# One core, four layers: paired maximum units on two row halves, earlier key and value projections, an earlier first expert

## The reference

```python
x = x + tanh(g_xattn[0]) * L0_xattn(layernorm(x), ctx)   # 16 heads of 16, causal: first 100 context rows
x = x + tanh(g_ffn[0])   * L0_ffn(layernorm(x))          # 8 experts, best one, and a shared one
x = x + tanh(g_xattn[1]) * L1_xattn(layernorm(x), ctx)   # latent attention, below
x = x + tanh(g_ffn[1])   * L1_ffn(layernorm(x))          # self attention, then 32 experts, best 8, and a shared one

def L1_xattn(hidden_q, kv_c):
    q_hk  = (hidden_q @ Wq.T).reshape(B, S, 16, 128)
    q_big = rope(einsum('bshk,hkq->bshq', q_hk, w_kc_q))
    kv_r  = rope(kv_c)                                   # 8 x 1444 x 64
    scores = einsum('bhsr,bhlr->bhsl', einsum('bshq,hqr->bhsr', q_big, W_qr),
                                       einsum('bld,hdr->bhlr', kv_r, W_kr))
    attn  = softmax(scores)                              # 16 heads x 100 queries over 1444 keys
    ctx_c = einsum('bhsl,bld->bhsd', attn, kv_r)
    return (ctx_lat(ctx_c, w_kc_kv)) @ Wo.T
```

## Time and profile before

| what | value |
|---|---|
| median of 3 runs | 1599.77 us (1599.54 to 1603.27) |
| profiled execution | 1590.53 us |
| its span, first to last instruction | 1588.8 us |
| mean granted TensorE clock | 0.944 of full speed |
| PE busy | 1470.2 us (93%), 7316 products |
| PEld busy | 1102.4 us (69%) |
| DVE busy | 899.7 us (57%) |
| ACT busy | 620.0 us (39%) |
| POOL busy | 781.4 us (49%) |
| DMA | 88.61 MB, mean 56 GB/s |

### The profile page before, as it was taken

How to read it: one execution, slowest core, us unless ns; L and a number is a source line. 1 busy time by engine, 2 the same in 40 slices (tenths; PEclk the granted TensorE clock), 3 DMA queues, 4 the chain that set the end, 5 groups by cost and what they waited for, 6 DMA issues and landing times. The chain is left out here.

```text
span 1588.8 us, 20773 instructions
## 1 busy us (share of the span) xinstructions
PE 1470.2 (93%) x7316; PEld 1102.4 (69%) x7316; DVE 899.7 (57%) x1581; ACT 620.0 (39%) x1117; POOL 781.4 (49%) x605
## 2 busy tenths in 40 slices
PE   7898999899978999999999998978999998799998
PEld 4586565544445766766766665567988877799998
DVE  1573111255556676786776763567878774444444
ACT  2243121133341344344343342356666653333333
POOL 0760102135544897797797764057465541233332
PEclk7798999699997999999999999789999998899999
DMA  8004111611001010110110000200110001343441
GB/s 301 1 1 146 51 47 38 212 48 49 1 11 55 29 57 4 54 57 1 57 57 1 19 1 2 81 27 10 46 54 2 27 1 41 105 122 121 121 121 51
DMA packets 60317, 88.61 MB, mean 56 GB/s; under 512 B 7556, under 2 KB 44612, under 8 KB 60230
## 3 DMA queue, kind: packets, MB, share of 16 engines
q1 hardware_dynamic: 59206, 85.82, 16.9%
q0 software_dynamic: 1024, 1.64, 0.4%
HBM read 81.92 MB, written 5.41 MB: 55 GB/s over the span
## 5 line engine op out<-in xcount | busy, mean ns | idle before, releaser
L965 ACT ACTIVATE prob<-PS 121x800 f32<-121x800 f32 x192 | 158.3, 838 | 248.8 <-PE PS L1937 246.0
L1344 DVE TENSOR_REDUCE mx<-PS 128x1 f32<-128x482 f32 (+1 forms) x312 | 185.6, 649 | 44.7 <-PE PS L1917 43.5
L618 POOL TENSOR_TENSOR e_wl<-e_wf,e_wh 128x768 fp32r<-128x768 f32 x33 | 70.8, 2144 | 181.0 <-ACT e_wh L883 159.1
L695 POOL TENSOR_TENSOR hT<-hT,prob 121x800 f32<-121x800 f32 x56 | 109.3, 1951 | 66.4 <-ACT prob L965 64.3
L1916 PE MATMUL PS<-kth,qs 128*128 128x482 f32 (+1 forms) x312 | 128.6, 412 | 13.4 <-DVE kl L1337 5.8
L1952 PE MATMUL PS<-prob,kvn 121*64 121x400 f32 (+1 forms) x768 | 136.1, 503 | 0.9 <-ACT prob L965 0.9
L695 POOL TENSOR_TENSOR xc<-xc,prob 121x800 f32<-121x800 f32 x56 | 117.7, 2101 | 13.6 <-ACT prob L965 8.3
L1917 PE MATMUL PS<-kl,qm 66*128 66x482 f32 (+1 forms) x312 | 122.5, 393 | 0.0
L1934 PE MATMUL PS<-qs,kth 128*121 128x400 f32 (+1 forms) x384 | 111.6, 373 | 7.8 <-DMA qm<-nml 4.8
L1937 PE MATMUL PS<-qm,kl 66*121 66x400 f32 (+1 forms) x384 | 103.8, 352 | 0.0
L1952 PEld LDWEIGHTS PS<-prob,kvn 121*64 121x64 f32 (+1 forms) x768 | 52.3, 137 | 71.2 <-issue 68.6
(11 more groups left out here) (278 smaller groups left out, 3565.9 us busy)
## 6 DMA issues: line engine op xcount, KB each, us to landing
e_wb<-routing SPq DMA_DIRECT2D x32, 400.0 KB, 3.9
wgu<-in_L_ffn_gate_up_proj SPq DMA_DIRECT2D x8, 1024.0 KB, 14.0
krt<-in_ctx_T SPq DMA_DIRECT2D x8, 722.0 KB, 4.1
ksw<-in_ctx_Tswap SPq DMA_DIRECT2D x8, 722.0 KB, 5.7
wdn<-in_L_ffn_down_proj SPq DMA_DIRECT2D x8, 512.0 KB, 7.9
wq<-in_L_ffn_Wq SPq DMA_DIRECT2D x4, 1024.0 KB, 5.1
wo<-in_L_ffn_Wo SPq DMA_DIRECT2D x4, 1024.0 KB, 5.5
e_wf<-in_L_ffn_Wg SPq DMA_DIRECT2D x32, 128.0 KB, 2.2
```

The source lines that it names most:

```text
L618: pool.tensor_tensor(m["wl"][:, slot], m["wf"][:, slot], m["wh"][:, slot].bitcast(fp32), ALU.subtract).then_inc(ms["wlo"], 1)
L695: pool.tensor_tensor(acc, acc, prob[:, n % RING], ALU.add).then_inc(xb["ap"], 1)
L965: act.activation(prob[0:k, n % RING], PS[0:k, 2 * (n % 2):2 * (n % 2) + 2, 0:GC], ACT.Exp).then_inc(xb["ex"], 1)
L1344: dve.tensor_reduce(mx3[:, m, g:g + 1], PS[:, 4 + k % 3, 0:SEG[g][1]], AX.X, ALU.max).then_inc(xb["free"], 1)
```

## The change

1. Units go in pairs. `queries_keys` takes one or two units: first their high products, then their low ones. `qm2` and `kl2` now have 128 rows, the same content in rows 0 to 63 and 64 to 127, and the second unit's low product reads rows 64 to 127. The low products of units have 64 rows in place of 66. So that the two score rows still exist, DVE sets rows 64 and 65 of `kl2` to one after each batch's maxima (before: once), ACT copies the queries twice (before: once), and `keep` falls away.
2. `UNITS` has more even steps, and in steps 8 and 14 a pair stands behind `values`.
3. The key and value projections move into the first norm, where PE, ACT and DVE have them between the norm's own steps; the context and its weights are loaded ahead of x. POOL expands the first three units of keys and one of values before the attention's stage, and clears `vx` there. The tanh of the gates moves from ACT's first place to behind the query copies.
4. The stage `ST_RT1` is gone. PE goes from the logits straight into the first expert's two `hidden`, turns the routing and opens the sums behind them; ACT keeps the routing between the first expert's gates; DVE waits for the spread routing at the first product that needs it. Logits and turned routing use banks 6, 4 and 5.

```diff
-        kl2 = sb("kl2", [DC + 2, 2, SK], fp32r, stack=st3)
-        qm2 = sb("qm2", [DC + 2, 2, HQ], fp32r, stack=st3)
+        kl2 = sb("kl2", [P, 2, SK], fp32r, stack=st3)
+        qm2 = sb("qm2", [P, 2, HQ], fp32r, stack=st3)
-        UNITS = (0, 0, 0, 0, 2, 4, 6, 8, 11, 14, 16, 18, 21, 24, 27, 30, 31, 33, 36, 39, 39, 39, 39, 39, 39)
+        UNITS = (0, 0, 0, 0, 2, 4, 6, 8, 10, 14, 16, 18, 20, 23, 25, 29, 31, 33, 36, 39, 39, 39, 39, 39, 39)
...
 # SP
+            sp.dma_start(c0T[:], a["ctx0T"]).then_inc(ld_x, 16)
+            sp.dma_start(wkv0T[:], a["L0_xattn_WkvT"]).then_inc(ld_x, 16)
             for c in range(NC):
                 sp.dma_start(xT[:, c, :], ...).then_inc(ld_x, 16)
...
 # ACT
-                act.activation(qm2[:, b % 2], qs[0:DC + 2, b].rearrange("p h s -> p (h s)"), ACT.Copy,
-                               scale=keep[:, 0:1]).then_inc(xb["q2"], 1)
+                src = qs[0:DC, b].rearrange("p h s -> p (h s)")
+                act.activation(qm2[0:DC, b % 2], src, ACT.Copy).then_inc(xb["q2"], 1)
+                act.activation(qm2[DC:P, b % 2], src, ACT.Copy).then_inc(xb["q2"], 1)
...
 # DVE
-                dve.tensor_tensor(kl2[0:DC, b % 2, cols], krt[0:DC, cols], kth[0:DC, b % 2, cols].bitcast(fp32),
+                dve.tensor_tensor(kl2[:, b % 2, cols], krt[:, cols], kth[:, b % 2, cols].bitcast(fp32),
                                   ALU.subtract).then_inc(xb["kl"], 1)
...
                 dve.tensor_tensor(nml[:], PS[0:MT, 4 + k % 3, 0:P], nmh[:].bitcast(fp32), ALU.subtract).then_inc(xb["free"], 1)
+                dve.memset(kl2[DC:DC + 2, b % 2].bitcast(fp32), 1.0).then_inc(xb["one"], 1)
...
 # PE
-                bank = PS[:, next_slot((xb["free"], next(freed))), 0:SEG[g][1]]
-                mm(bank, qs[...][:, cols], kth[:, b % 2, keys], start=True, stop=False)
-                mm(bank, qm2[:, b % 2, cols], kl2[:, b % 2, keys], start=False, stop=True).then_inc(xb["fill"], 1)
+                for u in units:
+                    ...
+                    banks.append(PS[:, next_slot((xb["free"], next(freed))), 0:SEG[g][1]])
+                    mm(banks[-1], qs[...][:, cols], kth[:, b % 2, keys], start=True, stop=False)
+                for i, u in enumerate(units):
+                    ...
+                    rows = slice(DC * i, DC * i + DC)
+                    mm(banks[i], qm2[rows, b % 2, cols], kl2[rows, b % 2, keys], start=False, stop=True).then_inc(xb["fill"], 1)
+
+            def unit_pairs(b, first, end):
+                for u in range(first, end, 2):
+                    queries_keys(b, range(u, min(u + 2, end)))
...
+            means(xT)
+            (4 key products)
+            variances("n0")
+            pe.wait_ge(ns["xc"], 2)
+            values_in(0, 0)
+            values_in(1, 1)
+            pe.wait_ge(p0["ke"], 2 * NC)
+            spread("n0")
+            values_in(2, 6)
+            values_in(3, 7)
...
                         hidden(m, ms, n, k, j, va + j, q, first and k < 2)
+                        if first and k == 1:
+                            routing_turned()
+                            open_sums()
```

175 lines of the change are left out of this document (87 added, 88 removed).

## The result

The changed kernel takes 1736.13 us (median, 1733.84 to 1738.68) where the kernel before, on the same chip, takes 1600.74 (1599.54 to 1603.27): 1.0837 of its time, 95% interval 1.0808 to 1.0866. Slower was forecast, by 25 us; it is 135 us, far outside the range (1592 to 1646). Ratios here compare executions in the same state, which leaves out two far ones, 2403.87 us in `xb_front` (granted clock 0.551) and 3629.33 us in `wait_long`.

What follows compares the result with a forecast made beforehand. PE was taken to bound the latent attention from batch 1 on. Latent attention +37, first stages -6 and first expert -6 gave +25 on 1590.5, 1615.5; with 9.3 carried over, 1625 us, range 1608 to 1642 (8 in 10: 1592 to 1646).

Steps and rivals of the forecast that it cites:

- From batch 1 on PE sets the pace: Latent attention: PE is busy 59.50 of 62 us, so a unit's cost on PE is its cost to the kernel.
- The price of a pair: Latent attention: a pair takes 1.07 us in place of 0.88, low products side by side, 0.20 us per change of form.
- form free: Rival: changes of the array's form cost nothing here, so pairs save time; 1571 us, chance 0.13.
- not side by side: Rival: the low products on row halves don't overlap, 0.21 us more a pair; 1652 us, chance 0.09.
- +27: Latent attention: pairs and single units cost +24 and +8 us, less 5 where column halves already paid a change.
- PE's waits for maxima go, since DVE's work stays: -5: Latent attention: PE's 5.4 us of waits for DVE's maxima vanish because PE's steps get longer.
- Batch 0's own units: Start of latent attention: 1.6 us a pair with three banks, 31 us in place of 23; +8, bounds 0 and 16.
- The second copy: Latent attention: ACT's second query copy delays key segments and first maximum, +1.0 us a batch; +7, bounds 0 and 11.
- The clock: No term of its own; a lower or higher clock only in the bounds for batch 0 and the first stages.
- The first stages: Before the latent attention: moving key and value projections into the first norm gives -6 us, bounds -10 and +1.
- The first expert: Last expert layer: first `down` comes 6 us earlier, at 1365.5 in place of 1371.77; -6, bounds -8 and -3.
- the chances for slower: Whole kernel: chance 0.79 of slower by more than 5 us, summed from 0.68, 0.09 and a third of 0.10.

Runs made afterwards that it cites:

- xb_front: Kernel before with parts 1 and 2 of the change, but the pairs of steps 8 and 14 ahead of the values; 1.065 of the time before.
- wait_long: Kernel before with one more PE wait a batch, in step 10 for ACT's exponential, lengthened by an idle ACT copy of 1.6 us; 1.0058.
- front_early: `xb_front` with the two query copies in steps 0 and 1 in place of step 2; 1.0401 of the time before.
- pairs66: Kernel before with two high, then two low products of 66 rows, the new `UNITS`, one query copy, nothing behind the values; 1.028.
- copy_early: Kernel before with the single copy of the next batch's queries in step 0 in place of step 2; 1.0085.
- xb_only: Kernel before with parts 1 and 2 of the change alone; 1.0901 of the time before.
- block_between: `xb_only` with DVE's step 8 block (reciprocals, product, sum) between the first two units' maxima and those of the pair behind the values; 1.0544.
- pairs66_oldtab: `pairs66` with the `UNITS` table of the kernel before; 1.0139 of the time before.
- rows64: Kernel before with 64 rows in place of 66 in every unit's low product, nothing else changed; 1.095.
- start_only: Kernel before with part 3 of the change alone; 1.0024 of the time before.
- expert_only: Kernel before with part 4 of the change alone; 0.9977 of the time before.
- no_pairs: Kernel before with parts 3 and 4 of the change, latent attention as before; 0.9959.

## Why the prediction was wrong, step by step

**"From batch 1 on PE sets the pace."** Right as a reading of the earlier trace rows, wrong as a rule to calculate by. The 62 us held only while DVE's work in steps 2 and 8 lay under something, and while the clock stayed up.

**The price of a pair: right.** 1.06 us measured, 1.07 forecast; the low products do run side by side, and the changes cost 0.19 each. The rivals "form free" and "not side by side" fall. `front_early` against `pairs66` gives 1.2% or 19 us (6 to 33) where +27 stood. That is not the form alone: `front_early` also has the second copy and the copies in steps 0 and 1, and moving one copy there cost 14 us by itself (`copy_early`). No run has the form and nothing else on top of `pairs66`.

**"PE's waits for maxima go, since DVE's work stays: -5": this step failed first.** I set PE's longer steps against DVE's work and never asked what stands in DVE's queue between the maxima. `behind`, which is in the diff, moved two units past the values, so DVE's maxima moved past them too and its block of 6 us lost its cover. In the place of -5 stand 40 us (`xb_only` less `xb_front`, 23 to 57; 56 in the profiles, and 57 in `block_between`). And pairs by themselves bring waits: the sum on DVE stands behind the maxima of two units, and PE's sums wait for it, 2.1 us in `pairs66_oldtab` and 1.2 in the changed kernel.

**Batch 0's own units: +8, bounds 0 and 16; measured 19.** The loop was right (the second high product waits for the pair before), but the whole of it ran at half clock, 2.22 us a pair in place of 1.6. Why the clock stayed down there is open: the order alone (`pairs66`) and the change of form alone (`rows64`) each do it, where the single units of before were at full clock after 7 us. Together with the waits of order and table this is the 45 us of `pairs66`, which has no change of form.

**The second copy: +7, bounds 0 and 11; alone it is 18 (13 to 23); with the pairs, moving both copies out of step 2 gave 40 (23 to 57).** The wait was foreseen, about 1.2 us a batch more; what follows it was not.

**The clock.** The prediction has it only in the bounds of batch 0 and of the first stages. In the changed kernel it is at half for 157 of the 488 us from the second negative maxima to the eighth and for 78 us in batch 0. Before it was 31 us in the same stretches. By the share of above, 0.24 to 0.36 of 235 - 31 = 204 us, some 50 to 75 us are the clock's, a third to a half of the loss, and no term of the sum had it. That is an estimate from `front_early`'s batches, and batch 0 may have another share; no run kept the waits and took the slower clock away.

**The first stages: -6 forecast.** The changed kernel's profile shows +1.5 at the end of the second norm, but so read the number is misleading. With the first stages of before, 15 profiles end that norm at 143.3 to 151.5, 147.6 on average, and the profile of before, 143.4, is the second shortest of them; with the new ones five profiles end it at 143.9 to 145.6, 144.6 on average. By these averages the gain is 3 us; the times of `start_only` show none (-2 to +9 us). About half of what was to be saved went into the first norm: the queries start at 30.61 us in place of 25.13, 5.5 later, where the load and the values had 1.4 + 1.5. The means start at 6.89 to 7.86 us in three profiles with the context ahead and at 5.07 to 5.98 in 15 without, 1.9 later on average. What took the rest stays open, since loading x first did not end the second norm earlier.

**The first expert: -6 forecast, right.** The last logits and experts take 248.9 to 252.6 us in 15 profiles with the old code, 250.0 on average, and 243.3 in five with the new, though the first `down` came 9 us earlier; the times of `expert_only` alone give -4 (-9 to +1).

**The sum.** Taken one on top of the other, the experiments give: order and table 45 us (`pairs66`; 3 net forecast, -5 and +8), the change of form with early copies 19 (`front_early` over it; 27), the copies in step 2 40 (`xb_front` over that; 7), the pairs behind the values 40 (`xb_only` over that; 0), together 144; the start and the first expert -7 (`no_pairs`; -12). That makes 137 against 134 measured. The four steps add up to `xb_only` by their construction, so the agreement checks only that the parts of the change add; how the 144 is shared among the four hangs on the order in which they are taken (the second copy is 18 by itself and 40 here). Each step carries some 15 us of uncertainty, and each includes the half clock that it brings. A slip besides: the chances for slower add up to 0.80, not 0.79.

## What to carry to other kernels

Where one engine is busy 95% of a steady stage, write down for each other engine what stands in its queue between the results that the busy one needs, and under what it lies: an edit that moves the need past that cover turns it into a wait. Price a wait of the matrix engine by its length and by the slower clock behind it. Compare a stretch with several profiles of the same code before calling a few us a loss or a gain.

## What the runs showed of the hardware

**Half clock behind a wait.** I counted PE's waits of 0.7 us and more from 555 to 985 us in the traces of before, of the changed kernel and of the 18 experiments, those that began at full clock and had no other such wait within 6 us. Half clock (0.5) began in or right behind 1 of 16 waits of 0.7 to 1.0 us, 5 of 12 of 1.0 to 1.6, 21 of 29 of 1.6 to 2.0, 33 of 38 of 2.0 to 2.6, and 17 of 17 longer ones. Like waits of neighbouring batches fall on either side. It then lasted 3.4 to 20.5 us. A wait is not the only place where the clock is low: in batch 0 of `rows64` it stayed at half for 99 us, 52 of them without a wait of PE.

**DVE beside POOL.** DVE's low keys of one segment take 0.64 us at the least, 1.08 in the median before and 2.34 in `copy_early`; one sum of 113 x 800, 1.0 us in the median, took 6.99 beside a POOL that was busy 6.86 of 7.00 us (`pairs66`, 649.2 us). The maxima, which read PSUM, have a median of 0.65 in all four (before, changed, `pairs66`, `copy_early`). "SBUF — State Buffer" of the Trainium skill, Who interferes with whom, says that a DVE instruction with two SBUF inputs contends with a GpSimd instruction that reads SBUF, and that the order of issue decides who blocks. The traces agree with the first (2.34 in place of 0.64 us); the second no run here isolates. So moving another engine's instruction, as `copy_early` does, can lengthen these.

**The change of form in both directions.** 0.10 before and 0.10 behind it, at 64 rows of 482 columns, 0.19 a change in a row of them, and 0.30 at half clock. Products of 66 rows pay none of it (0.22 from start to start). "TensorEngine Tiling (Array Packing)" of the Trainium skill, Key Properties, has the drain; the price is from `rows64`.
